# The first layer rebuilt as one software pipeline, and the zero fills issued by GpSimd from a smaller tile

## What is computed

```
# layer 0: queries = layernorm(x), keys = values = ctx; 8 heads of 4 features
q, k, v = heads(LN(x) @ Wq + bq), heads(ctx @ Wk + bk), heads(ctx @ Wv + bv)
x += merge(softmax(q k^T * scale) v) @ Wo + bo
h = LN(LN(x)) * gamma + beta
probs = softmax(clip(h @ Wr.T)); top 2 of 8 experts, at most 640 tokens each
x += sum over the 2 of prob * W3[e] @ (silu(W1[e] @ h) * (W2[e] @ h))      # d_ff 1024
# layer 1: the same shape with 16 heads of 16 features,
# top 3 of 15 experts of width 256 and one shared expert of width 512; x is the output
```

## Time and profile before

| | us |
|---|---|
| median of three executions | 1615.44 (1612.3 to 1617.35) |
| the profiled execution, span from first to last instruction | 1607.1 |
| layer 0 up to the experts | 0 to 363 |
| experts of layer 0 | 363 to 739 |
| project of layer 1 | 739 to 847 |
| the rest of layer 1 | 847 to 1607 |

### The profile page before, as it was taken

The page is one execution under the profiler, slowest core; times in us unless marked ns, Lnnn a source line. Parts: engine busy times, 40 slices in busy tenths (PEclk is TensorE's granted clock), DMA queues, the critical chain, the costliest instruction groups (busy, mean ns, idle before and its releaser), DMA issues. The chain is left out here.

```text
span 1607.1 us, 20254 instructions
## 1 busy us (share of the span) xinstructions
PE 1256.6 (78%) x6250; PEld 810.2 (50%) x6251; DVE 788.3 (49%) x1610; ACT 549.8 (34%) x1053; POOL 376.1 (23%) x370
## 2 busy tenths in 40 slices
PE   7559983617999999997847999998861899999910
PEld 5202343507999999995421333336730455555500
DVE  0558717425555566644167888842430113444423
ACT  1407640314434444430132666661230102233200
POOL 3010003773222233304230000000037000111156
PEclk9859986567999999996575999998786899999965
DMA  4264310343322223204132222105412202222234
GB/s 107 80 220 140 131 37 18 101 159 128 112 83 95 92 71 107 96 17 133 28 107 77 60 61 60 59 8 176 160 50 104 102 0 73 84 82 82 71 88 136
DMA packets 110635, 144.43 MB, mean 90 GB/s; under 512 B 26618, under 2 KB 90464, under 8 KB 108902
## 3 DMA queue, kind: packets, MB, share of 16 engines
q1 hardware_dynamic: 98038, 101.62, 20.2%
q0 software_dynamic: 12528, 41.94, 7.6%
HBM read 95.10 MB, written 48.76 MB: 90 GB/s over the span
## 5 line engine op out<-in xcount | busy, mean ns | idle before, releaser
L682 DVE TENSOR_REDUCE M<-S 128x1 f32<-128x512 f32 x384 | 248.7, 685 | 71.4 <-PE S L534 67.7
L659 ACT ACTIVATE PT<-S 128x1024 f32<-128x1024 f32 x192 | 196.1, 1025 | 103.0 <-PE S L553 102.8
L534 PE MATMUL S<-KS,QS 96*128 96x512 bf16 x384 | 162.2, 427 | 47.1 <-DMA KS<-scrk 20.5
L534 PEld LDWEIGHTS S<-KS,QS 96*128 96x128 bf16 x384 | 38.7, 101 | 188.9 <-DVE M L682 139.0
L1044 POOL TENSOR_TENSOR w12l<-stage,w12h 128x1024 fp32r<-128x1024 f32 x32 | 77.5, 2425 | 202.6 <-ACT w12h L1038 202.5
L1620 PE MATMUL H<-W,XST 128*128 x248 | 121.8, 614 | 2.1 <-issue 0.9
L553 PE MATMUL S<-QS,KS 98*128 98x512 bf16 x384 | 117.0, 389 | 8.0 <-DMA QS<-NM 5.0
L1220 DVE TENSOR_TENSOR HTm0l<-HFm,HTm0h 128x320 fp32r<-128x320 f32 x128 | 122.3, 956 | 1.0
L565 PE MATMUL PV<-PT,VG 128*32 128x512 f32 x768 | 101.9, 608 | 7.8 <-ACT OSB L640 7.8
L1226 DVE TENSOR_TENSOR HFm<-Um,SGm 128x320 f32<-128x320 f32 x128 | 62.3, 486 | 78.9 <-ACT SGm L1189 78.5
L521 POOL COPY VG<-VA 128x512 f32<-128x512 f32 (+1 forms) x24 | 14.7, 613 | 362.2 <-PE PV L565 334.0
(11 more groups left out here) (240 smaller groups left out, 2491.1 us busy)
## 6 DMA issues: line engine op xcount, KB each, us to landing
stage<-in_W12T SPq DMA_DIRECT2D x32, 512.0 KB, 6.1
xs<-zeros POOLq DMA_DIRECT2D x12, 1024.0 KB, 7.3
QS<-scrq SPq DMA_DIRECT2D x144, 64.0 KB, 2.2
KS<-scrk SPq DMA_DIRECT2D x144, 64.0 KB, 2.3
stage<-in_W3T SPq DMA_DIRECT2D x16, 512.0 KB, 3.9
XS<-xs SPq DMA_DIRECT2D x62, 128.0 KB, 2.0
ys<-YS POOLq DMA_DIRECT2D x62, 128.0 KB, 2.0
W<-in_fc1T SPq DMA_DIRECT2D x2, 3840.0 KB, 22.2
```

What stands on the lines that cost most here:

```text
L534: pe.matmul(S1[:, q % 2, :], QS[0:ROWS, slot, h, q * P:(q + 1) * P], KS[0:ROWS, slot, h, :], start=True, stop=True).then_inc(s1_ready, 1)
L659: act.activation(PT[:, c % 2, h, 2 * u:2 * u + 2, :], S2[:, u, :, :], ACT.Exp, scale=lay.scale).then_inc(exp_done, 1)
L682: dve.tensor_reduce(M[:, c % 2, h * TPB + q:h * TPB + q + 1], S1[:, q % 2, :], AX.X, ALU.max).then_inc(max_done, 1)
```

## The change

`project`, `attend` and `route0` of layer 0 are replaced by one block, `layer0`. It has 102 beats. In beat t each engine does a short list of steps for tile t of the attention (64 tiles of 2 heads x 128 rows: 8 groups of 8) and side steps of other stages, chosen by `tasks(t)`. The maxima run `AHEAD` = 14 beats in front of the scores. The 8 heads have 4 features, now not padded: 24 rows (26 with the shift rows) of a 32-row strip for each head, and the stacks are built on TensorE (`stacks`, a product with 0/1 selections) and never go to HBM. The two pairs of PSUM banks named S1 are a ring (`Ring`) that maxima and all side steps take in turn. Output projection, norms, router and ranks follow sequence by sequence, 18 to 32 beats behind. The normalization uses a power on GpSimd in place of a square root on ScalarE.

The keys of layer 1 are no longer projected in layer 0 but in `project` of layer 1. The zero tile has 256 rows, so `xs0` is filled by 20 DMAs and `xs1` by 31. The 20 are issued by GpSimd in the first beats. The 31 are issued after the last scatter; they are waited for at the end of `experts0`. The weights of the experts are two tiles, the second allotted only in `experts0`, where XS and YS have tiles of their own.

```
-ZROWS = 1024
+ZROWS = 256
...
-        split_of = "q" if experts else "kq"
+        split_of = "kq"
...
+AHEAD = 14
...
+    T_END = NC0 + LA + 24
...
+        def ends(b):
+            return 16 * b + 18 + LA
...
+            found = [("stack", 2 * b + g) for b in range(1, BATCH) for g in range(2) if t == 16 * b - 8 + 4 * g]
+            found += [("v", b) for b in range(BATCH) if t == (2, 5, 38, 54)[b]]
+            found += [("xnt", b) for b in (2, 3) if t == 2 * b]
+            found += [("qk", 1)] if t == 12 else []
+            for b in range(BATCH):
+                e = ends(b)
+                found += [(n, b) for n, d in (("ont", 3), ("out", 5), ("xft", 8), ("router", 10), ("rank", 14)) if t == e + d]
+            return found
...
+            def maxima(c):
...
+                for j in range(2):
+                    at = slice(VW * (h + j), VW * (h + j) + SH0)
+                    m = pe.matmul(out[:, j, :], QS[at, n % 4, q * P:(q + 1) * P], KS[at, n % 4, :], start=True, stop=True)
+                m.then_inc(S1.filled(("max", c)), 1)
...
+            def scores(s):
...
+                for j in range(2):
+                    wait(pe, exp_done, 2 * s + j - 1)
+                    pe.matmul(S2[:, j, :], KS[rows(h + j), n % 4, kt * P:(kt + 1) * P], QS[rows(h + j), n % 4, :],
+                              start=True, stop=True).then_inc(s2_ready, 1)
...
+            for t in range(T_END):
+                s = t - LA
+                if t < NC0:
+                    maxima(t)
...
+                if 0 <= s < NC0:
+                    scores(s)
+                if s >= 3 and (s - 3) % 2 == 0 and (s - 3) // 2 < TPB * NG0:
+                    values(*divmod((s - 3) // 2, TPB))
+                if s >= 12 and (s - 12) % BEATS0 == 0 and (s - 12) // BEATS0 < NG0:
+                    turn_out((s - 12) // BEATS0)
+                for name, b in tasks(t):
+                    side[name](b)
...
+            def fill(dram, rows_, done):
+                for r in range(0, rows_, ZROWS):
+                    k = min(ZROWS, rows_ - r)
+                    pool.dma_start(dram[r:r + k, :].rearrange("(p a) d -> p (a d)", p=P), zeros[:, 0:k * D // P]).then_inc(done, 16)
+
+            fill(env.xs0, E0 * CAP0, filled0)
...
+                    if t == e + 15:
+                        scatter(b)
+            fill(env.xs1, TILES1 * P, filled1)
+            for b in range(BATCH):
+                pool.wait_ge(scattered[b], 16 * TPB * K0)
...
             pairs(pool, expert)
+            pool.wait_ge(env.filled_rows[1], 16 * -(-TILES1 * P // ZROWS))
```

More of the change, by code:

```diff
@@ L1045, in load_weights_low, with __init__, take, filled @@
                            ALU.subtract).then_inc(ew.low_done, 1)
+AHEAD = 14
+HD0, H0 = 4, 8
+W0 = H0 * HD0
+NG0 = BATCH * H0 // GH
+BEATS0 = 8
+NC0 = BEATS0 * NG0
+SH0 = HD0 * len(Q_TERMS)
+NR0 = SH0 + SHIFT
+SLICES = 4
+class Ring:
+    def __init__(self, sem, name, tiles):
+        self.tiles, self.n = tiles, len(tiles)
+        self.ready = [sem(f"{name}_ready{i}") for i in range(self.n)]
+        self.free = [sem(f"{name}_free{i}") for i in range(self.n)]
+        self.at = {}
+    def take(self, pe, task):
+        i = len(self.at)
+        assert task not in self.at
+        self.at[task] = i
+        wait(pe, self.free[i % self.n], i // self.n)
+        return self.tiles[i % self.n]
+    def filled(self, task):
+        return self.ready[self.at[task] % self.n]
+    def full(self, eng, task):
+        i = self.at[task]
+        eng.wait_ge(self.ready[i % self.n], i // self.n + 1)
+        return self.tiles[i % self.n]
+    def emptied(self, eng, task):
+        i = self.at[task]
+        eng.wait_ge(self.free[i % self.n], i // self.n + 1)
+    def done(self, task):
+        return self.free[self.at[task] % self.n]
@@ L1049, with load_low @@
+def load_low(pool, ew, e, c):
+    pool.wait_ge(ew.high_done, piece_at(e, c) + 1)
+    pool.tensor_tensor(ew.part(1, 0, c), ew.stage[:, c % STAGES, :], ew.part(0, 0, c).bitcast(F32),
+                       ALU.subtract).then_inc(ew.low_done, 1)
 PASSES = ((0, 0), (0, 1), (1, 0))
@@ L1160, in expert @@
                             m = pe.matmul(Y[:, (s * NTE + i) % 2, 0:D], HT[a][:, j, i * P:(i + 1) * P],
-                                          ew.w3[b][:, s, j, :], start=(j == 0 and (a, b) == PASSES[0]),
+                                          ew.w3[b][s][:, j, :], start=(j == 0 and (a, b) == PASSES[0]),
                                           stop=(j == FB - 1 and (a, b) == PASSES[-1]))
@@ L1765, in program @@
         env.filled, env.scattered = sem("filled"), sem("scattered")
+        env.filled_rows = [sem(f"filled_rows{i}") for i in range(2)]
+        env.scattered_rows = [sem(f"scattered_rows{b}") for b in range(BATCH)]
         env.gathered = [sem(f"gathered{i}") for i in range(GDEEP)]
@@ L1794, in program @@
             sb, _, sem = scope(nc, first)
-            attention(sb, sem, lay0)
+            env.zeros = sb("zeros", [P, ZROWS * D // P])
             env.EW = Weights(sb, sem)
-            route0(nc, env, ins, lay0, lay1)
+            layer0(nc, env, ins)
             experts0(nc, env, ins)
```

772 lines of the change are left out of this document (595 added, 177 removed).

## The result

The changed kernel takes 1607.01 us (median of 9 runs, 1602.34 to 1610.49), the kernel before 1615.44 on the same chip (9 runs, 1610.55 to 1620.0). The ratio is 0.9948 with a 95% interval of 0.9931 to 0.9964: 8 us faster, where 45 were forecast. The profiled execution has a span of 1603.4 us against 1607.1.

A forecast was written before the change was run, and what follows sets the result against it. Layer 0's three stages under-used the machine, with room in the seams and routing block. Layer 0 -66, layer 1's keys +19, fill data +2 give -45: span 1562, time 1570 us; own range 1550 to 1595, full range 1530 to 1640.

The forecast's parts named there:

- beats 0 to 13: Layer 0's first beats, maxima alone with side steps, priced at half clock: 35 us.
- beats 14 to 63: Layer 0's middle 50 beats: TensorE longest at 2.3 us a beat, times 1.25, so 2.86 a beat, 143 us.
- beats 64 to 77: Layer 0's last beats: scores, value steps, one router chain, bound by 14 x 2 exponentials and handovers: 25 us.
- last exponentials to last scatter: End of layer 0: the last sequence's chain, for 4 tiles and not 16, with 8 scatters: 45 us.
- keys in `project` of layer 1: Layer 1's keys delay the additions of gathered rows and the next gathers: 19 us lost, bounds 3 and 24.
- the clock from beat 14 on at 0.9 or more: Sign of the forecast in layer 0: TensorE's clock at least 0.9 and TensorE busy 80%; at 0.5 the half-clock rival holds.
- the low clock as a rival: TensorE stays at half clock in layer 0, as maxima and scores have fewer rows: 4.45 us a beat, 1678 us; chance 0.17.
- the third rival: Layer 0's pairs of maxima overlap and coupling is mild: 0.22 us less a beat, 50 beats in 120, 1540 us; chance 0.20.
- The fills: 17 us on the path: End of layer 0: GpSimd issues 31 DMAs at 0.551 us while all engines wait: 17.1 us.
- The data of the 31 ... bounds 0 and 8: The fills' 7.9 MB still arrives when the experts load their first rows: 2 us added, bounds 0 and 8.
- The fourth rival: The 31 fills hold GpSimd at the pace of their data, 24 us: costs 7 more, inside the forecast; no chance given.
- the rule that I weighed: Batches of 1 MiB or more speak against 256 KB fills; the sum stayed, since nobody waits for their data until experts' end.

The follow-up runs named there:

- four full products: Changed kernel with four unread 128-row products ahead of the two maxima of each beat of layer 0: 1605.52 us, ratio interval 0.9916 to 0.9978.
- the interleaved kernel: Changed kernel with xs1's fills moved into layer 0's first two experts and keys and values alternating by sequence in layer 1's project: 1561.9 us, ratio 0.9670.
- the kernel with the bias on GpSimd: Kernel with interleaved keys and values, layer 1's value bias added by GpSimd, not TensorE: 1491.22 us, ratio 0.9513; in layer 0 too: 1485.34 us, 0.9467.

## Why the prediction was right or wrong

Right: faster, and inside the range. Wrong: the gain was 8 us and not 45. Term by term, forecast and measured, in us:

| term | forecast | measured |
|---|---|---|
| until the first maxima | 30 | 31.1 |
| beats 0 to 13 | 35 | 40 |
| beats 14 to 63 | 143 | 156 |
| beats 64 to 77 | 25 | 37 |
| last exponentials to last scatter | 45 | 46 |
| fills and handover | 19 | 29 |
| layer 0 | 297 | 339 |
| keys in `project` of layer 1 | +19 | +18.1 |

The 42 us of layer 0 are nearly the whole error: the forecast span was 1562, the measured is 1603.4. (The forecast had 2 us more for the data of the fills, which the measured 29 contain.)

The step that failed is "Beats 14 to 63: 143 us", whose prices are those of full clock, with its sign "the clock from beat 14 on at 0.9 or more". The granted clock was 0.56, in rows as busy as those of old attention at 1.00, and TensorE's work was 2.87 us a beat (143.67 / 50) where I had 2.3. The term missed by 13 us only, by luck: I had multiplied the work by 1.25 for handovers, and at 92% busy they came to 1.09. With 1.09 the forecast would have been 125, and 31 us are what the clock cost in these 50 beats after what the overlap of the pairs gave back, an estimate from these numbers. The last 14 beats took 12 us more than forecast at 0.59; how much of that is the clock's, no run parts. Beats 0 to 13 I had priced at half clock already, so their 5 us are not the clock's; no run shows whose they are.

I had the low clock as a rival and gave it 0.17. The first argument against it was that the value steps fill the array for a third of the time. By my own sum it was a fifth (7.3 of 36.6); in the trace it is 30% (L1102, 43.2 of TensorE's 143.7 us), and the clock stayed low; it rose when full products were added. The second, that old attention "kept 1.00 throughout", was wrong by the earlier trace rows (0.85 for the stage; 1.00 is from 124 to 198 us), and no argument: its products had 96 and 98 rows, and these were the ones the change made thin.

That rival's time, 1678, was 71 us too long, by the mechanism of the third rival, the overlap of the pairs: I gave it 4.45 us a beat with one product after the other, and the pairs of maxima ran at the same time (0.40 for two at 1.2 GHz, 0.23 with the clock up). The Trainium skill, page TensorE: Matmul & The Clock Gate, section Part 3: Packing small matmuls, says so of products of 32 rows or fewer in different row groups, and the trace agrees for the 24-row maxima; of the scores (26 rows) a pair held 0.56 us, partly overlapped. At full clock my 2.3 us of TensorE work a beat stands well: with four full products (0.97) a beat took 3.21, which leaves 2.24. So the mistakes went against each other. By this estimate (no run had the full clock without the added products) the clock cost up to 1.2 us a beat (3.44 against 2.24), and against the rival's 4.45 the overlap gave back, with 0.92 for two at half clock one after the other, 0.92 - 0.40 for the maxima and 0.92 - 0.56 for the scores, 0.9 us, which leads to 3.55 where 3.44 were measured.

The Trainium skill, page TensorE: Matmul & The Clock Gate, section Part 1: The HAM clock gate, has the clock follow how busy TensorE has been. Here 50 us at 99.7% busy stayed at 0.50 (the value stretch of `project`), and 156 us at 92% at 0.56: busy time alone does not tell the clock.

The second step that failed is "The fills: 17 us on the path", and "The data of the 31 ... bounds 0 and 8". I let the block end when GpSimd had issued them; it ended 3.7 us after the last had landed (issued at 326.1, and the longest took 9.3 to land: 335.4), 29.0 us after the last scatter. The fourth rival had the right mechanism, 24 us at the pace of the data, and I put it aside as small. That no instruction waits for a DMA inside a block does not mean that the block's end does not. The 31 of 256 KB moved at 350 GB/s (315 to 330 us), and the fills of 1 MB of the kernel before, beside the loads of the stacks, at 380 and 347 for all (83 to 93 and 93 to 104 us). So the rule that I weighed (the Trainium skill, page DMA: Bandwidth & Descriptors, section Bandwidth, batches of 1 MiB or more) would have set no price here: issued back to back on one queue, the small ones showed no loss.

The keys were sized right (18.1 and, moved alone, 18.3, forecast 19) and for the reason given: VectorE's key units held the gathers (43.9 us for the 17th). In another order, with keys, the last root came at 74.8, no later than before without them (76.7). The reduction of 1024 columns took 1.222 us, forecast 1.22. Some 4 us more were lost behind `project`, where TensorE's idle time for the shared expert's first layer (L2008) is 46.4 us and was 41.9 before. I did not look into what moves it.

What stays open: how the clock chooses between 1.2 and 2.4 GHz. The runs show that products of 128 rows raise it in layer 0, and that in `project` one-row products keep it from rising. What holds it down in layer 0 was not isolated: taking out the one-row bias products alone did not raise it, and no run leaves out the small side products (router, ranks, transposes) or makes the maxima and scores fuller without adding work. The last 14 beats were seen once at a higher clock, 35.2 us at 0.68 where the trace beside it had 40.5 at 0.55: two traces, no more.

## What to carry to other kernels

When a rewrite makes TensorE's products thinner, price it at half clock first, whatever the busy share says, and count products in different row strips as one. Where a stretch of values stays at half clock, take the one-row bias products off TensorE: in `project` 50 us became 19, and GpSimd adds the bias while nobody waits for it. In layer 0, with products of 24 rows beside them, it did not raise the clock. Put bulk DMAs of the software queue where no block ends behind them, and put independent work between dependent steps in the order of every engine's list, not all of it first.

## What the runs showed of the hardware

- TensorE 92 to 100% busy at a granted clock of 0.50 to 0.56 for 50 and 156 us; added products of 128 rows raised it in steps to 0.66, 0.80 and 0.93, added products of 24 rows left it at 0.57 (one trace of a kernel whose runs differ).
- Value tiles with a one-row product each ran at full clock for 6.6 us behind full products, and at half clock for 6.3 us after TensorE had stood 3.6 to 4.6 us.
- Two products of 24 rows in different row strips held TensorE 0.40 us at half clock and 0.23 at full, as long as one.
- A block in which GpSimd had only issued DMAs ended 3.7 us after the last had landed (335.4 to 339.1), 12.4 us after the last issue.
- On one of the chips the kernel before ran in 1569.1 us and not 1615. No trace of it is from that chip; set beside each other, the interleaved kernel needs 762 us from the first reduction of layer 1's attention to the end and the kernel with the bias on GpSimd, on that chip, 718. TensorE's idle time before the shared expert's first layer is 42.5 us in the one trace and 3.2 in the other, and ScalarE's first Gelu, for which it waits 60.5 us in the changed kernel's trace while GpSimd issues its 48 scatters, has no such wait on that chip. Why is open.
